# Attention across heads of the last batch, moved from the first part's queues into those of the layers

## The reference

```
x = x + attention(conditioning(x, ids, states))          # 16 heads of 16, softmax over 256 tokens
x = x + layers(modulated(x, cond_512))

def modulated(x, s):                  # attention across the heads of one token
    kx = modulated_linear(x, s, k_w)           # (8, 256, 16 heads, 16)
    A = softmax(einsum('bnhd,bnjd->bnhj', kx, kx) / 4)
    out = einsum('bnhj,bnjd->bnhd', A, kx)
    return modulated_linear(out, s, o_w)

def layers(x):                        # 6 of them, 16 heads of 64, windows of 64 tokens
    x = local_attention(shift(x)) @ Wo + x
    x = gated_ffn(layernorm(shift(x))) + x
```

## Time and profile before

| | us |
|---|---|
| median of three runs | 3293.62 |
| lowest and highest | 3293.61, 3301.92 |
| the profiled execution's own time | 3300.11 |
| its span, from the first to the last instruction | 3298.8 |
| PE busy | 3077.8 (93%) |
| DVE, ACT, POOL busy | 2645.4, 2534.9, 2082.1 |

### The profile page before, as it was taken

One profiled execution on the slowest core, in us unless ns is written; L12 is line 12 of the kernel. 1 busy time (PEld: TensorE's weight loads), 2 busy tenths in 40 slices (PEclk: granted clock), 3 DMA queues, 4 the chain that ended last, 5 costly groups with the idle time before them and its releaser, 6 DMA issues. The chain is left out here.

```text
span 3298.8 us, 80718 instructions
## 1 busy us (share of the span) xinstructions
PE 3077.8 (93%) x29936; PEld 2726.8 (83%) x29936; DVE 2645.4 (80%) x5117; ACT 2534.9 (77%) x7059; POOL 2082.1 (63%) x1536
## 2 busy tenths in 40 slices
PE   5888886489999999999999999999999999999997
PEld 4666664379998999998999989999899998999996
DVE  3378988678888888889878898878988878888874
ACT  2787884278787888787878788878788888888884
POOL 5357645666666666667666666666666667676661
PEclk7898996699999999999999999999999999999999
DMA  3111100100000000001000011000100000000000
GB/s 127 55 39 55 49 4 7 41 25 22 2 2 22 32 30 2 1 11 42 30 2 2 3 36 40 7 2 2 37 25 22 2 2 21 33 29 8 5 8 26
DMA packets 27780, 75.04 MB, mean 23 GB/s; under 512 B 4120, under 2 KB 9848, under 8 KB 27256
## 3 DMA queue, kind: packets, MB, share of 16 engines
q1 hardware_dynamic: 22224, 52.63, 5.0%
q0 software_dynamic: 4864, 16.78, 1.6%
q10 hardware_dynamic: 304, 0.47, 0.1%
HBM read 65.68 MB, written 4.19 MB: 21 GB/s over the span
## 5 line engine op out<-in xcount | busy, mean ns | idle before, releaser
L1577 POOL TENSOR_TENSOR turned<-by_cos,turned 128x512 f32<-128x512 f32 x384 | 492.9, 1284 | 843.5 <-DVE turned L2032 843.2
L1581 POOL TENSOR_TENSOR rnorm<-norm,half 128x8 f32<-128x8 f32 x384 | 788.1, 2052 | 0.0
L1835 ACT ACTIVATE prob<-ps_s,ebias,rnorm 128x128 f32<-128x128 f32 x1536 | 682.1, 457 | 62.3 <-DVE ebias L2053 61.6
L2046 DVE TENSOR_REDUCE negmax<-ps_s 128x8 f32<-128x1024 f32 x192 | 235.1, 1225 | 290.6 <-PE ps_s L1658 290.2
L1844 ACT ACTIVATE prob_t<-ps_t 128x512 f32<-128x512 f32 x384 | 230.0, 599 | 226.6 <-PE ps_t L1667 221.9
L2061 DVE TENSOR_TENSOR prob<-prob,rinv 128x512 f32<-128x512 f32 x384 | 376.0, 979 | 13.1
L1604 PE MATMUL ps_qk<-w_hi,x_hi 128*128 128x512 f32 x768 | 336.2, 438 | 18.3 <-DVE turned L2032 9.8
L1743 PE MATMUL ps_f<-hid_hi,w_hi 128*128 128x256 f32 (+1 forms) x1056 | 309.1, 293 | 5.7 <-DVE hid_lo L2107 5.6
L1835 ACT ACTIVATION_READ_ACCUMULATOR prob<-ps_s,ebias,rnorm 128x1 f32 x1536 | 311.4, 203 | 0.0
L1604 PE MATMUL ps_qk<-w_lo,x_hi 128*128 128x512 f32 x768 | 304.5, 396 | 0.0
L1604 PE MATMUL ps_qk<-w_hi,x_lo 128*128 128x512 f32 x768 | 303.8, 396 | 0.0
(11 more groups left out here) (289 smaller groups left out, 9763.0 us busy)
## 6 DMA issues: line engine op xcount, KB each, us to landing
w_raw<-in_w_qkv SPq DMA_DIRECT2D x24, 768.0 KB, 4.6
w_raw<-in_w SPq DMA_DIRECT2D x12, 693.0 KB, 3.9
w_raw<-in_w_o SPq DMA_DIRECT2D x12, 512.0 KB, 3.3
w_raw<-in_w SPq DMA_DIRECT2D x6, 768.0 KB, 4.4
x_tok<-in_x SPq DMA_DIRECT2D x8, 256.0 KB, 2.7
kept<-x_t SPq DMA_DIRECT2D x8, 256.0 KB, 2.0
w_raw<-kept SPq DMA_DIRECT2D x8, 256.0 KB, 2.9
out<-rows_out SPq DMA_DIRECT2D x8, 256.0 KB, 3.1
```

The lines of the kernel that those rows point to most:

```text
L1577: G.tensor_tensor(turned[:, k, :], by_cos[:, :], turned[:, k, :], ALU.add).then_inc(s["turned"], 1)
L1581: G.tensor_tensor(rnorm[:, i % RR, :], norm2[:, k, :], half[:, :], ALU.pow).then_inc(s["rnorm"], 1)
L1835: last = A.activation(prob[:, k, h, :], half_bank(h % 2, k)[:, T(h // 2)], ACT.Exp, bias=ebias[:, i // NU % 2, k, h:h + 1], scale=rnorm[:, ...
L2046: V.tensor_reduce(negmax[:, k, :, :].rearrange("p u (c o) -> p o u c", o=2), ps_s[:, :, :].rearrange("p o (u c k) -> p o u c k", u=NU, c=2 ...
```

## The change

The front's queues leave out attention across heads of batch 7, from `turn_k` and `head_prod` on; `token_k` of batch 7 stays. The front has 131 steps in place of 139. The functions go by `late` to `local_layers`, which puts them for c = 7 into the queues of the same engines at steps 0 to 15, by `lates(t, off)`. Their tiles must outlive the front, so they are allocated first, and so are the tiles of the feed-forward's weights (w1, w2) in the layers, which lie at the same place and are written only after step 15. Three waits guard the order: `w_o_mm` of pass 0 for o2_t (both use the same bank), `mean_mm` and `w1_high` for state, `take_x` of batch 7 for its state. The wait for the tables' transfers (dma_c) goes from the head of the PE and DVE queues to `score` and to `tables`, behind `take_x`. The zeros in w2_hi are made in `w2_low` of layer 0.

```diff
     m = {}
+    m["kx"], m["kd"] = sb("kx", [P, NU, D]), sb("kd", [P, 2, NU, HD, NH])
+    m["prod"], m["prodo"] = sb("prod", [P, 2, 4 * NH * HD]), sb("prodo", [P, 2, 4, HD, NH])
+    m["sc"], m["scm"] = sb("sc", [P, 2 * NU, NH, NH]), sb("scm", [P, NH])
+    m["scs"], m["scr"] = sb("scs", [P, NH]), sb("scr", [P, NH])
+    m["o2"], m["o2_t"] = sb("o2", [P, NU, D]), sb("o2_t", [P, KT, N])
+    m["o_w"] = sb("o_w", [P, KT, D])
+    m["fcols"] = sb("fcols", [P, 16 + NTILE + 3 * KT])
+    m["style"] = sb("style", [P, 4, B])
+    m["dem"] = sb("dem", [P, 4 * B])
+    m["zero"] = sb("zero", [P, 1])
     m["SB"] = ctx.enter_context(nc.psum_tensor("bank_scores", [P, 4, 512], F32))
     for bank in ("PB", "OB", "M0", "M1"):
...
-FRONT_STEPS = 139
+FRONT_STEPS = 131
...
+    def heads(t, off):
+        return due(t, off, HP, B - 1)
...
-            for q in batches(t, 74):
+            for q in heads(t, 74):
                 turn_k(q)
-            for q in batches(t, 80):
+            for q in heads(t, 80):
                 head_out(q, 1, 1)
...
+
     sp()
-    pool()
-    pe()
-    act()
-    dve()
+    late = {"pool": pool(), "pe": pe(), "act": act(), "dve": dve(), "o2_t": s["o2_t"], "ostate": s["ostate"]}
     nc.all_engine_barrier()
+    return late
...
+    w1_hi, w1_lo = sb("w1_hi", [P, KT, HID]), sb("w1_lo", [P, KT, HID])
+    w2_hi, w2_lo = sb("w2_hi", [P, NJ, D]), sb("w2_lo", [P, NJ, D])
     w_hi, w_lo = sb("w_hi", [P, KT, NG, 3 * GC]), sb("w_lo", [P, KT, NG, 3 * GC])
     wo_hi, wo_lo = sb("wo_hi", [P, INNER // P, D]), sb("wo_lo", [P, INNER // P, D])
-    w1_hi, w1_lo = sb("w1_hi", [P, KT, HID]), sb("w1_lo", [P, KT, HID])
-    w2_hi, w2_lo = sb("w2_hi", [P, NJ, D]), sb("w2_lo", [P, NJ, D])
...
+    def lates(t, off):
+        return [B - 1] if t == off else []
...
-        G.wait_ge(s["lset"], 5)
+        G.wait_ge(s["lset"], 6)
...
         for t in range(STEPS):
+            for c in lates(t, 6):
+                head_out(c, 0, 1)
+            for c in lates(t, 6):
+                head_out(c, 0, 2)
+            for c in lates(t, 15):
+                head_out(c, 1, 3)
             for i in units(t, 3):
                 rotated(i)
+            for c in lates(t, 8):
+                head_out(c, 0, 3)
...
+            for c in lates(t, 1):
+                turn_k(c)
+            for c in lates(t, 4):
+                head_out(c, 0, 0)
+            for c in lates(t, 13):
+                head_out(c, 1, 2)
...
+            for c in lates(t, 10):
+                head_out(c, 1, 0)
+            for c in lates(t, 10):
+                head_out(c, 1, 1)
...
+            else:
+                E.wait_ge(s["dma_c"], 48)
...
+                if q == 0:
+                    E.wait_ge(late["o2_t"], B)
...
             E.wait_ge(s["lx1"], q + 1)
...
+            else:
+                E.wait_ge(late["ostate"], B)
...
-        E.wait_ge(s["dma_c"], 48)
...
+            for c in lates(t, 14):
+                heads_out(c)
             for i in units(t, 0):
                 project(i)
...
+            for c in lates(t, 13):
+                flip_heads(c)
...
+            else:
+                A.wait_ge(late["ostate"], B)
...
             for i in units(t, 4):
                 soften(i)
+            for c in lates(t, 2):
+                head_mirror(c, 0)
...
+            for c in lates(t, 2):
+                head_exp(c, 0)
...
+            for c in lates(t, 8):
+                head_exp(c, 1)
...
+            for c in lates(t, 5):
+                head_mirror(c, 1)
             for i in units(t, 0):
                 project(i)
...
+            for c in lates(t, 15):
+                heads_out(c)
...
+            for c in lates(t, 13):
+                flip_heads(c)
...
         def tables(layer):
...
+            if layer == 0:
+                V.wait_ge(s["dma_c"], 48)
...
 
         def w2_low(layer):
...
+            if layer == 0:
+                V.tensor_scalar(w2_hi[REST:P, NJ - 1, :].bitcast(F32R), raw(NJ * D)[REST:P, (NJ - 1) * D:], 0.0, None, ALU.mult)
...
+            if r == B - 1:
+                V.wait_ge(late["ostate"], B)
...
-        V.wait_ge(s["dma_c"], 48)
-        V.tensor_copy(w2_hi[REST:P, NJ - 1, :].bitcast(F32R), hidden[REST:P, NJ - 1, :])
...
+            for c in lates(t, 1):
+                head_prod(c, 0, 3)
...
+            for c in lates(t, 7):
+                head_peak(c, 1)
...
+            for c in lates(t, 4):
+                head_scores(c, 1, 1)
...
                 soften(r)
             for i in units(t, 1):
                 rotate(i)
+            for c in lates(t, 9):
+                head_out(c, 1, 0)
...
+            for c in lates(t, 2):
+                head_peak(c, 0)
+            for c in lates(t, 13):
+                head_out(c, 1, 2)
+            for c in lates(t, 4):
+                head_out(c, 0, 1)
...
             for i in units(t, 5):
                 weigh(i)
+            for c in lates(t, 0):
+                head_prod(c, 0, 0)
+            for c in lates(t, 8):
+                head_weights(c, 1)
+            for c in lates(t, 0):
+                head_prod(c, 0, 1)
+            for c in lates(t, 4):
+                head_scores(c, 1, 2)
+            for c in lates(t, 2):
+                head_prod(c, 1, 0)
+            for c in lates(t, 3):
+                head_scores(c, 1, 0)
+            for c in lates(t, 0):
+                head_scores(c, 0, 0)
+            for c in lates(t, 3):
+                head_out(c, 0, 0)
+            for c in lates(t, 0):
+                head_scores(c, 0, 1)
+            for c in lates(t, 4):
+                head_prod(c, 1, 3)
+            for c in lates(t, 13):
+                head_out(c, 1, 3)
...
+            for c in lates(t, 1):
+                head_scores(c, 0, 2)
...
+            for c in lates(t, 9):
+                head_out(c, 1, 1)
+            for c in lates(t, 4):
+                head_scores(c, 1, 3)
...
+            for c in lates(t, 2):
+                head_prod(c, 1, 1)
+            for c in lates(t, 0):
+                head_prod(c, 0, 2)
+            for c in lates(t, 8):
+                head_out(c, 0, 3)
...
+            for c in lates(t, 2):
+                head_weights(c, 0)
...
+            for c in lates(t, 3):
+                head_prod(c, 1, 2)
...
+            for c in lates(t, 7):
+                head_out(c, 0, 2)
+            for c in lates(t, 1):
+                head_scores(c, 0, 3)
...
```

More of the change, by code:

```diff
@@ L352, in pool @@
                 gather(q, 0)
-            for q in batches(t, 75):
+            for q in heads(t, 75):
                 head_out(q, 0, 3)
@@ L376, in pool @@
                 scale_h(q)
-            for q in batches(t, 79):
+            for q in heads(t, 79):
                 head_out(q, 1, 0)
@@ L667, in pe @@
                 dem_flip(_)
-            for q in batches(t, 82):
+            for q in heads(t, 82):
                 flip_heads(q)
@@ L925, in act @@
                 slots(q, 0, 0)
-            for q in batches(t, 73):
+            for q in heads(t, 73):
                 head_mirror(q, 1)
@@ L951, in act @@
                 inv_rows(q)
-            for q in batches(t, 71):
+            for q in heads(t, 71):
                 head_exp(q, 0)
@@ L955, in act @@
                 slots(q, 1, 0)
-            for q in batches(t, 68):
+            for q in heads(t, 68):
                 head_mirror(q, 0)
@@ L959, in act @@
                 flip_x(q)
-            for q in batches(t, 81):
+            for q in heads(t, 81):
                 heads_out(q)
@@ L1311, in dve @@
                 x_stats(q)
-            for q in batches(t, 66):
+            for q in heads(t, 66):
                 head_prod(q, 0, 3)
@@ L1373, in dve @@
                 y_add(q)
-            for q in batches(t, 67):
+            for q in heads(t, 67):
                 head_scores(q, 1, 0)
@@ L1598, in pe @@
         E = nc.tensor
+        flip_heads, heads_out = late["pe"]
         def times_wqkv(out, g, u, columns):
@@ L1801, in act @@
         A = nc.scalar
+        head_mirror, head_exp, flip_heads, heads_out = late["act"]
         def project(i):
@@ L1956, in dve @@
         V = nc.vector
+        head_prod, head_scores, head_peak, head_weights, head_out = late["dve"]
         def heads(ap):
```

77 lines of the change are left out of this document (38 added, 39 removed).

## The result

On the first chip the changed kernel takes 3273.97 us in the median of 4 runs (3269.31 to 3281.66), the kernel before 3296.55 us in 4 (3293.61 to 3301.92): ratio 0.9931, 95% interval 0.9913 to 0.9949, that is 22.6 us or 0.7% faster. On a second chip it was measured once more beside the last experiments: 3272.36 us in 6 runs against 3301.61 in 11, ratio 0.9918 (0.9897 to 0.9939). The forecast was 16.6 us faster, the range 3264 to 3290 us.

A forecast was written before the change was run, and what follows sets the result against it. It took PE to bound the later layers and a ring through DVE, POOL and PE their first steps. 34.3 us gained in front less 17.7 late made 16.6 faster, 3293.6 to 3277 us; range 3264 to 3290.

The forecast's parts named there:

- 17.7 of 26.8 as lateness alone: Layers: batch 7's moved work adds 26.8 us on DVE; the units come 17.7 us late, with port and clock.
- Front, 34.3: Front: without batch 7's attention across heads, state of batch 6 ends at 582.3 instead of 616.6 us, 34.3 us gained.
- The copied paces: End of front: batch 6 takes batch 7's pace, 10.5 us from weights to last o-reduce, 7.1 more to state.
- Step 0, rotate(0) late by 1.1: Layers' first step: project starts some 2.5 us sooner, but tables and DVE's products make rotate(0) 1.1 us late.
- Steps 1 to 4, late by 10.0: Early layers: reduces, peak, products and weights on DVE ahead of rotate; lateness grows from 2.2 to 10.0 us.
- Steps 7 to 15, to 13.7: Later steps: weights, o-reduces and short PE and ACT operations, partly hidden in waits, bring lateness from 10.0 to 13.7 us.
- Port, 2 of 0 to 17: Steps 2 to 8: POOL slows eight two-input DVE operations through the shared read port; 2 us taken from 0 to 17.
- The rival built on a meeting for each: Steps 2 to 8: POOL holds each of eight two-input DVE operations 2.1 us; 1.6 us faster, 3292 us; chance 0.15.
- Clock, 2 of 0 to 6: Start of the layers: PE may stay longer at the 1.2 GHz clock; 2 us taken from 0 to 6.
- What would show it: Signs in the profile, such as 16th unit's project 110 to 117 us after the layers' first instruction, o-reduces at 1.21 us.
- hidden: Layers: most of the moved DVE work falls in idle time, late by 6 us at best, 3265 us; chance 0.15.
- in series: Steps 2 to 9: all DVE and POOL work comes onto the ring, late by 46.8, 12.5 slower, 3306 us; chance 0.03.

The follow-up runs named there:

- the second execution: The changed kernel profiled once more, unchanged, on a second chip; 3272.36 us in the median of 6 runs there, ratio 0.9918.

## Why the prediction was right, and where its terms were off

The direction, the size and the mechanism hold: DVE saturated the first part of the layers, PE the rest, and the late work was paid in part: 11.3 to 13.8 us of DVE's 26.6 were, about half, where I had 17.7 of 26.8 as lateness alone, about two thirds. In the profiled spans, 18.4 us shorter: kx 3.4 us later by chance, 32.55 gained, 12.15 late at unit 20, 3.1 back by the tiles' places, 1.7 more behind the last unit. Without the two parts that other executions did not repeat this is 23.5 us (26.2 by the second execution), near the 22.6 of the first medians and the 27 of the second chip's ratio, against 16.6. Part of the nearness is luck: the front was put 1.8 us too high, the lateness 5.6 to 8.0 us too high, and 3.1 us of gain stood nowhere in the sum. By steps:

- **Front, 34.3: measured 32.55.** The estimate of "some 2 us of exp and small operations" for head_weights left out that the peak's subtraction meets POOL's product. The copied paces were exact.
- **Step 0, rotate(0) late by 1.1: 0.39.** Project starts 5.20 us after L, where it was 7.12 (1.9 sooner, 2.5 forecast): x_hi took 1.26 us beside turn_k, which began at 589.47 us and took 2.37, and 0.42 without it. That the gain of the wait is spent by DVE's products held; without the late work unit 0 is 2.76 sooner.
- **Steps 1 to 4, late by 10.0: 7.34.** Step 1's reduces cost 0.3, not 1.1; step 2 cost 2.2 where I had 2.8, steps 3 and 4 4.4 where I had 5.0. DVE's waits took up more of the work than the two of 1.6 us that I gave them.
- **Steps 7 to 15, to 13.7: 9.67 to 12.15.** From unit 4 to 10 it grows by 2.4 us (forecast 2.7). That the o-reduces of steps 13 to 15 fit in waits was right; the 1 us for TensorE's and ACT's short operations there stays open: the second execution goes from 9.88 to 9.66, but against a kernel before that lost 1.1 us of its own at these units, so that up to 1 us may be in it.
- **Port, 2 of 0 to 17: 1.6, of which part was hidden.** In steps 2 to 8 two two-input operations were held, one of them (0.69 in place of 0.17 us) for the softmax, and this one, with POOL's product beside it since 638.29 us:

```profile
635.14 1.00 DVE L2130 TENSOR_TENSOR prob<-prob,rinv 128x512 f32<-128x512 f32 x1
...
639.10 2.12 DVE L2130 TENSOR_TENSOR prob<-prob,rinv 128x512 f32<-128x512 f32 x1
```

  All eight late products ran at their free pace, as the groups above show. Four of them met no operation of POOL. The other four lay beside `rnorm`, the power of 8 elements in `rotated`, which takes about 2 us: the first two rows show it for products of 1024 and 768. The third row shows what the sum had nowhere, that POOL is held too:

```profile
607.28 1.83 POOL L1600 TENSOR_TENSOR rnorm<-norm,half 128x8 f32<-128x8 f32 x1
607.53 2.08 DVE L1259 TENSOR_TENSOR prod<-kx 128x1024 f32<-128x1024 f32 x2
...
616.59 2.14 POOL L1603 TENSOR_TENSOR turned<-turned,rnorm 128x256 f32<-128x256 f32 x1
```

  The last takes 0.61 us in most units; here it began 0.1 us after DVE's w_lo (1.76 us), and TensorE's flip_qk waited 1.62 us for it. The rule of the Trainium skill, SBUF — State Buffer, section "Who interferes with whom", that two SBUF inputs on DVE and a reading POOL operation block one another, agrees with the 2.12 and the 2.14 us. It does not agree with the product inside `rnorm`, which reads tiles in SBUF too: 1.22 us, as if alone. The rival built on a meeting for each (3292 us) is out, but by luck of the order as much as by rule: with everything 1.2 us later, one meeting cost 4.1 us (the kernel with the reduces twice). The kernel before had its own, w_hi at 1.53 and 1.48 us, which are 0.95 here.
- **Clock, 2 of 0 to 6: next to 0 by unit 11, 0 to 2.5 later.** The low clock was there (0.50 in the first 15 us), but beside a full DVE; with DVE less full it was worth 1.2 us. Where it did cost was beyond the stretch I had in mind, at units 12 and 18, and not in every execution.
- **Not in the forecast: the tiles' places, 3.1 us.** The prediction treated the new order of the allocations as costless either way.
- **What would show it**: project of the 16th unit came 106.8 us after L (95.7 before), not 110 to 117, since the lateness was 11.1 there. State of batch 6 ended 26.2 us after kx (24.4 forecast), DVE was busy for 39.0 of the layers' first 40 us, o-reduces were at 1.21 us.

Of the rivals, "hidden" (late by 6) and "in series" (46.8) are both out, but the second had something: the two engines' late work is paid side by side, not one behind the other, yet up to unit 10 whatever is added beyond it counts nearly in full, as the doubled products show. The prediction's reason against it, POOL's 33 us idle, was no reserve: POOL's work of batch 7 alone costs 8.0 us by unit 10 and 10.5 by unit 20. That the gaps are waits in the ring, and products put into them push `rotated`, is my reading of it.

## What to carry to other kernels

An idle share of an engine in a ring of three engines is not room for work: ask what stands behind the new operation in its queue. When two engines of a ring each get extra work, the ring may pay about the larger of the two (here up to unit 8, the clock apart); what is then added to either is paid nearly in full, and a shift by 1 us can cost 4 where it brings two operations together that hold one another. Before work is moved into a saturated start, it should first fill the idle end of the part before it: there a quarter of it (6.3 of 26.8 us on DVE) cost nothing.

## What the runs showed of the hardware that was not expected

- The placement of tiles in on-chip memory alone changed the layers by 3.0 us in the 2470 from unit 20 to the last, spread evenly, with no instruction more or less.
- A cast of 1536 elements took 3.08 us and a subtraction 3.76 beside POOL's products, 0.95 and 1.76 without. POOL's copy of 512 elements took 1.05 us beside a reduce and 2.37 beside DVE's subtraction w_lo, and DVE's cast x_hi, one input, took 1.26 us beside that copy and 0.42 without it: holding goes both ways and does not need two inputs. The power `rnorm` on POOL (8 elements, 1.83 us) held neither of the two products beside it (2.08 us for both).
- The granted clock of two executions of the same kernel was alike in every window of 5 us for the first 85 us of the layers, within 0.02, and differed after that, which was worth 2.5 us.
